# Who makes the low halves of the rotated queries and keys: two of four moved from VectorE to GpSimd

## The reference

```python
qkv = x @ Wqkv.T                         # 512 x 768
q, k, v = split(qkv)                     # 16 heads of 16 features
q = cos * q + rotate_half(q) * sin
k = cos * k + rotate_half(k) * sin
scores = q @ k.T / 4, causal, softmax
out = (scores @ v) @ Wo.T
```

## Time and profile before

| | |
|---|---|
| median of 3 runs | 2299.27 us (2298.2 to 2305.56) |
| profiled execution | 2291.23 us, its span 2289.5 us, granted TensorE clock 0.989 |
| instructions | 52,899 |
| busy: PE / DVE / ACT / POOL | 2109.5 (92%) / 1931.8 (84%) / 1354.4 (59%) / 1306.6 (57%) us |
| DMA queue | 291.90 MB, 50.3% of 16 engines |

### The profile page before, as it was taken

The page is one execution under the profiler, slowest core; times in us unless marked ns, Lnnn a source line. Parts: engine busy times, 40 slices in busy tenths (PEclk is TensorE's granted clock), DMA queues, the critical chain, the costliest instruction groups (busy, mean ns, idle before and its releaser), DMA issues.

```text
span 2289.5 us, 52899 instructions
## 1 busy us (share of the span) xinstructions
PE 2109.5 (92%) x17682; PEld 1141.4 (50%) x17682; DVE 1931.8 (84%) x4485; ACT 1354.4 (59%) x2568; POOL 1306.6 (57%) x1462
## 2 busy tenths in 40 slices
PE   4999999889999999999999999999999888999999
PEld 2666666434444444444444444444444434666666
DVE  6777788788999899999989998999999865777776
ACT  3455444266667666666666676666666655445553
POOL 6666667454555455456545554554555425666664
PEclk9999999899999999999999999999999999999999
DMA  6656666444445444444444454444445423666665
GB/s 208 192 192 207 201 203 200 116 89 89 98 95 101 94 94 98 89 94 93 99 89 100 95 101 94 96 92 96 93 94 98 99 70 118 197 202 194 204 207 167
DMA packets 280391, 295.29 MB, mean 129 GB/s; under 512 B 45784, under 2 KB 263224, under 8 KB 280120
## 3 DMA queue, kind: packets, MB, share of 16 engines
q1 hardware_dynamic: 280120, 291.90, 50.3%
HBM read 140.08 MB, written 83.89 MB: 98 GB/s over the span
## 4 chain that ended last, share of the span: by engine, by line
PE 45%; DVE 33%; SPq 7%; issue 6%; DMA 5%; ACT 4%; DVEq 0%; ACTq 0%
PE bank L710 8%; DVE bank L996 7%; DVE at_mx L1006 7%; PE bank L728 7%; PE bank L1185 6%; PE bank L1202 6%; PE bank L1219 4%; PE bank L1280 4%; ACT probs L1073 3%; DVE turned L975 3%; DVE v_qk L981 3%; DVE turned L974 2%; DVE at_stats L107 2%; PE bank L1255 2%; PE bank L1167 2%
## 5 line engine op out<-in xcount | busy, mean ns | idle before, releaser
L1073 ACT ACTIVATE probs<-bank 128x512 f32<-128x512 f32 x1280 | 747.0, 603 | 456.9 <-PE bank L1185 447.5
L912 POOL TENSOR_SCALAR_AFFINE_SELECT probs<-probs 128x512 f32<-128x512 f32 x512 | 320.4, 638 | 661.1 <-ACT probs L1073 659.3
L1006 DVE TENSOR_REDUCE at_mx<-bank 128x1 f32<-128x384 f32 (+2 forms) x896 | 509.6, 608 | 78.5 <-PE bank L1167 77.0
L1185 PE MATMUL bank<-stacks 49*128 49x512 f16 (+3 forms) x2048 | 458.7, 302 | 71.4 <-ACT probs L1073 71.0
L996 DVE CUSTOM_DVE_ANT_0 bank<-bank,xn 128x512 f32<-128x512 f32 x512 | 351.6, 698 | 38.8 <-PE bank L1158 36.2
L1185 PEld LDWEIGHTS bank<-stacks 49*128 49x128 f16 x2048 | 136.0, 94 | 458.6 <-ACT probs L1073 334.2
L1162 PE MATMUL bank<-stacks 48*128 48x384 f16 (+2 forms) x1536 | 307.7, 275 | 22.1 <-DVE at_mx L1006 15.6
L1167 PE MATMUL bank<-mask,turn 64*128 64x128 bf16 (+2 forms) x896 | 230.7, 257 | 0.0
L1158 PE MATMUL bank<-stacks 48*128 48x512 f16 x512 | 198.5, 389 | 10.6 <-DVE at_mx L996 6.4
L924 POOL TENSOR_TENSOR turned<-turned 128x512 f32<-128x512 f32 x128 | 184.7, 1443 | 19.1 <-POOL turned L920 0.4
L628 ACT ACTIVATE turned<-bank,b1s 128x512 f32<-128x512 f32 x128 | 88.2, 689 | 181.0 <-PE bank L710 179.3
(11 more groups left out here) (145 smaller groups left out, 4619.6 us busy)
## 6 DMA issues: line engine op xcount, KB each, us to landing
stacks<-qk_image SPq DMA_DIRECT2D x384, 128.0 KB, 4.5
qk_image<-v_qk SPq DMA_DIRECT2D x128, 256.0 KB, 3.7
stacks<-w_hi SPq DMA_DIRECT2D x192, 128.0 KB, 3.7
stacks<-w_lo SPq DMA_DIRECT2D x192, 128.0 KB, 3.8
b2s<-in_b SPq DMA_DIRECT2D x128, 128.0 KB, 3.9
after_ffn<-probs SPq DMA_DIRECT2D x32, 512.0 KB, 6.5
at_x<-after_ffn SPq DMA_DIRECT2D x32, 512.0 KB, 4.1
late_x<-after_ffn SPq DMA_DIRECT2D x32, 512.0 KB, 4.7
```

What stands on the lines that cost most here:

```text
L912: nc.gpsimd.affine_select(out=ap, in_=ap, compare_op=ALU.is_ge, fill=0.0, base=0, pattern=[[0, d] for d in dims] + [[1, P]], channel_multi ...
L1006: nc.vector.tensor_reduce(o_ap, i_ap, AX_X, ALU.max).then_inc(max_done, 1)
L1073: nc.scalar.activation(probs[:, c, :], st_ps[c % 2][:], ACT.Exp, scale=DH ** -0.5).then_inc(exp_done, 1)
L1185: ins = nc.tensor.matmul(bank[:, col:col + T - q0], k_stack[ss.par][rows, j + ha, kt * P:(kt + 1) * P], q_stack[ss.par][rows, j + ha, q0:T ...
```

## The change

The low halves of t = 0, 1 (queries) become GpSimd instructions in slot 1, each right behind the rotation steps of t = 2 and t = 3. The low halves of t = 2, 3 (keys) stay on VectorE in slot 2. To make that possible `rotated` gets four buffers; by_sin goes (the product with sin is made in place in swapped), so that the memory stays the same. The semaphore qk_lo becomes q_lo and k_lo; other users of qk_lo follow (not shown: L503, L620, L785, L1334).

```diff
-        rope = [[self.turned[:, 2 * j + i, :] for i in range(2)] for j in range(4)]
+        rope = [self.turned[:, 0:2, :], self.turned[:, 2:4, :], self.turned[:, 4:8, :]]
@@ SP, slot
             if g == 1 and sample(s + 1):
-                hold(sp, issue, qk_lo, 4 * n.b + 2)
+                hold(sp, issue, q_lo, 2 * n.b + 2)
                 (write q)
             if g == 2 and sample(s + 1):
                 (read q)
-                hold(sp, issue, qk_lo, 4 * n.b + 4)
+                hold(sp, issue, k_lo, 2 * n.b + 2)
                 (write k)
@@ GpSimd
-            nc.gpsimd.tensor_tensor(by_sin[t % 2][:], swapped[t % 2][:], sin_t[:], ALU.mult).then_inc(sin_done, 1)
-            wait(pool, qk_lo, idx - 1)
+            nc.gpsimd.tensor_tensor(swapped[:, t % 2, :], swapped[:, t % 2, :], sin_t[:], ALU.mult).then_inc(sin_done, 1)
+            wait(pool, q_lo if t < 2 else k_lo, 2 * n.b)
             pool.wait_ge(sin_done, idx + 1)
-            nc.gpsimd.tensor_tensor(rotated[t % 2][:], by_cos[t % 2][:], by_sin[t % 2][:], ALU.add).then_inc(rope_done, 1)
+            nc.gpsimd.tensor_tensor(rotated[:, t, :], by_cos[:, t % 2, :], swapped[:, t % 2, :], ALU.add).then_inc(rope_done, 1)
+
+        def q_low(n, t):
+            pool.wait_ge(qk_hi, 4 * n.b + t + 1)
+            wait(pool, q_written, 32 * n.b)
+            nc.gpsimd.tensor_tensor(qk.lo[:, t, :], rotated[:, t, :], qk.hi[:, t, :], ALU.subtract).then_inc(q_lo, 1)
@@ GpSimd, slot: mask 0, then
             if g < 2 and sample(s + 1):
                 rope(s + 1, 2 * g)
+            if g == 1 and sample(s + 1):
+                q_low(s + 1, 0)
                 (slot 2: normalise s + 2), masks 1 to 3, then
             if g < 2 and sample(s + 1):
                 rope(s + 1, 2 * g + 1)
+            if g == 1 and sample(s + 1):
+                q_low(s + 1, 1)
@@ VectorE
-        def rope_low(n, t):
+        def k_low(n, t):
             dve.wait_ge(qk_hi, 4 * n.b + t + 1)
-            wait(dve, q_written if t < 2 else k_written, 32 * n.b)
-            nc.vector.tensor_tensor(qk.lo[:, t, :], rotated[t % 2][:], qk.hi[:, t, :], ALU.subtract).then_inc(qk_lo, 1)
+            wait(dve, k_written, 32 * n.b)
+            nc.vector.tensor_tensor(qk.lo[:, t, :], rotated[:, t, :], qk.hi[:, t, :], ALU.subtract).then_inc(k_lo, 1)
@@ VectorE, slot
-                if g in (1, 2) and sample(s + 1) and n in (0, 3):
-                    rope_low(s + 1, 2 * (g - 1) + (n == 3))
+                if g == 2 and sample(s + 1) and n in (0, 3):
+                    k_low(s + 1, 2 + (n == 3))
```

More of the change, by code:

```diff
@@ L502, in residual @@
             if before and s == 0:
-                pool.wait_ge(before.qk_lo, 4 * B)
+                pool.wait_ge(before.k_lo, 2 * B)
             if before and s == 2:
@@ L619, in gelu @@
                 act.wait_ge(before.pv_done, 16 * (B - 1))
-                act.wait_ge(before.qk_lo, 4 * B)
+                act.wait_ge(before.k_lo, 2 * B)
             if before and s == 1:
@@ L759, in attention @@
     cos_t, sin_t = sb("cos", [P, T], F32), sb("sin", [P, T], F32)
-    q_stack, k_stack, v, qk, (swapped, by_cos, by_sin, rotated), ones = mem.of_attention()
+    q_stack, k_stack, v, qk, (swapped, by_cos, rotated), ones = mem.of_attention()
     x = mem.at_x
@@ L784, in attention @@
     xT_lo, qk_done, rope_in, sin_done = sem("xT_lo"), sem("qk_done"), sem("rope_in"), sem("sin_done")
-    rope_done, qk_hi, qk_lo, v_done = sem("rope_done"), sem("qk_hi"), sem("qk_lo"), sem("v_done")
+    rope_done, qk_hi, q_lo, v_done = sem("rope_done"), sem("qk_hi"), sem("q_lo"), sem("v_done")
+    k_lo = sem("k_lo")
     v_copied, mx_done, max_done, mt_done = sem("v_copied"), sem("mx_done"), sem("max_done"), sem("mt_done")
@@ L973, in begin_rope @@
             wait(dve, rope_done, idx - 1)
-            nc.vector.tensor_tensor(by_cos[t % 2][:], x_ps[t % 2][:], cos_t[:], ALU.mult)
-            nc.vector.stream_shuffle(swapped[t % 2][:], x_ps[t % 2][:], [i ^ 1 for i in range(32)]).then_inc(rope_in, 1)
-        def rope_low(n, t):
+            nc.vector.tensor_tensor(by_cos[:, t % 2, :], x_ps[t % 2][:], cos_t[:], ALU.mult)
+            nc.vector.stream_shuffle(swapped[:, t % 2, :], x_ps[t % 2][:], [i ^ 1 for i in range(32)]).then_inc(rope_in, 1)
+        def k_low(n, t):
             dve.wait_ge(qk_hi, 4 * n.b + t + 1)
-            wait(dve, q_written if t < 2 else k_written, 32 * n.b)
-            nc.vector.tensor_tensor(qk.lo[:, t, :], rotated[t % 2][:], qk.hi[:, t, :], ALU.subtract).then_inc(qk_lo, 1)
+            wait(dve, k_written, 32 * n.b)
+            nc.vector.tensor_tensor(qk.lo[:, t, :], rotated[:, t, :], qk.hi[:, t, :], ALU.subtract).then_inc(k_lo, 1)
         def maxima(s, g, n):
@@ L1078, in rope_high @@
             wait(act, q_written if t < 2 else k_written, 32 * n.b)
-            nc.scalar.activation(qk.hi[:, t, :], rotated[t % 2][:], ACT.Copy).then_inc(qk_hi, 1)
+            nc.scalar.activation(qk.hi[:, t, :], rotated[:, t, :], ACT.Copy).then_inc(qk_hi, 1)
         def high_of(hi, n, c, ps_done, hi_done):
@@ L1332, in attention @@
     own.xT_lo, own.rope_in, own.stored = xT_lo, rope_in, stored
-    own.st_done, own.pv_done, own.qk_lo, own.k_written = st_done, pv_done, qk_lo, k_written
+    own.st_done, own.pv_done, own.k_lo, own.k_written = st_done, pv_done, k_lo, k_written
     own.max_done, own.on_done, own.xn_done = max_done, on_done, xn_done
```

## The result

The changed kernel takes 2366.44 us (median of 4 runs, 2362.96 to 2372.5), the kernel before 2298.73 us (4 runs): ratio 1.0309, 95% interval 1.0276 to 1.0342 (an estimate over the single runs; the quotient of the two medians is 1.0295). It is slower, as forecast, and 3 us from the forecast of 2363. Most of the steps held, but one term of the sum is too large, and another cost, not foreseen, made up for it: that the number fits to 3 us is luck.

A forecast was written before the change was run, and what follows sets the result against it. PE (45%) and VectorE (33%) held the chain, the next sample's DRAM path nearly as late. A loop of 26.4 + 20.7 = 47.1 us against 45.04 adds 31 x 2.06 = 64 to 2291.2: 2355, plus 8 for the median, 2363 us; range 2318 to 2400.

The forecast's parts named there:

- VectorE's relief: Slots 1 and 2: VectorE is late by about 1.1 us a sample; giving that back vanishes in PE's wait.
- POOL's subtraction: Slot 1: each q low half on POOL takes 1.28 us, bounds 0.64 and 1.76.
- Q: POOL's slot 1: both q low halves are complete at 1224.5, 26.4 us after the start of slot 0.
- The DMA path from Q: q reads start at Q + 3.1, k writes at Q + 6.0, k reads at Q + 12.6, landed at Q + 20.7.
- The loop's period: Slot 0 to Q to the next slot 0: 47.1 us against 45.04, +2.06 us a sample.
- The sign that the prediction named for itself: Start of slot 0: a new PE wait of about 2 us once a sample, between DMA L846 and PE L1158 or L1162.
- The collision of the keys' low half with L920 of t = 3: Slot 2: by the port rule POOL's L920 can hold VectorE's key low half for a full 1.1 us.
- Rival 1: The DMA path fits in a loop of at most 44 us and VectorE's time counts: 2265 us at best, chance 0.09.
- Rival 2: The loop just closes at 44.8 to 45.3 us: no measurable change, 2299 us, chance 0.06.
- Rival 3: Slot 2's row of maxima, queued behind q writes, is late for slot 3: up to 0.7 us, 2287 us, chance 0.03.
- Rival 4: POOL is much slower at mixed types, 2.5 us each: period 49.5, +138 us, 2437 us, chance 0.05.

The follow-up runs named there:

- early_low_k_late: early_low with the keys' low half of t = 2 on VectorE moved behind maximum n = 2 of slot 2 instead of n = 0: 2254.10 us, ratio 0.9834.
- path_away: Changed kernel, but the DRAM image's low half of q is written from the high halves and SP waits for those only: 2349.51 us, ratio 1.0253.
- k_late: Changed kernel with only the keys' low half of t = 2 on VectorE moved behind maximum n = 2 of slot 2: 2343.65 us, ratio 1.0194.
- path_away_k_late: path_away with the keys' low half of t = 2 on VectorE moved behind maximum n = 2 of slot 2: 2293.77 us, ratio 1.0006.
- early_low: Changed kernel with POOL's q low halves moved forward in slot 1, t = 0 ahead of the first mask, t = 1 right behind it: 2296.86 us, ratio 1.0011.
- late_write: Changed kernel with all low halves back on VectorE, and SP also waiting for slot 2's first mask before writing q: 2421.69 us, ratio 1.0538.

## Why the prediction was right, and where it was not

- **VectorE's relief** (1.1 us a sample, to vanish in PE's wait): right in size. 0.76 us appeared in slot 1 and were lost again; early_low_k_late, without the new waits, gets 1.06, of which 0.74 are the q low halves' and 0.32 the reordering's.
- **POOL's subtraction** (1.28 us taken): 1.16 us, the median of 51 in the steady stretch (1149 to 1169 ns). It is a little faster than the float32 instructions beside it (1.27).
- **Q, the end of the q low halves** (26.4 us after the start of slot 0): 1170.26 - 1144.54 = 25.7. Two subtractions 0.12 shorter each and a collision of 0.27 instead of 0.45 are about 0.4 of the 0.7.
- **The DMA path from Q** (3.1, 6.0, 12.6 and 20.7 us): q reads at 1173.33 = Q + 3.1, k write at Q + 5.9, k reads at Q + 12.5, landed at 1190.55 = Q + 20.3. The k writes, issued 1.2 us earlier behind the reads (2.8 us after the first read for 4.03), landed no earlier, as taken: 9.4 us after the first read. In the seven samples with full clock and a wait for the stacks, PE starts 20.4 to 20.9 us after Q.
- **The loop's period** (47.1 us, +2.06): 46.1 in the sample shown, 46.1 to 46.6 in those seven, so +1.1 to +1.6. This is the term that was mis-sized. In the sample shown the error is the sum of the two above, 0.7 at Q and 0.3 behind it, small in themselves but half of the difference of two large numbers.
- **The clock** was not in the prediction at all, and costs the rest: a mean of 47.58 against 46.3 at full clock. The forecast of 2363 hit 2366 because the missing term (about 1.3 us a sample) covered what the loop was too long by (0.5 to 1.0). That is luck. The sign that the prediction named for itself, a new wait of about 2 us for the stacks once a sample, did not come: nine waits in 1100 us, 6.1 us in all.
- **The collision of the keys' low half with L920 of t = 3** stood in the prediction as 1.1 us for VectorE by a rule, and then went into the sum only as 0.4 us for POOL. It happened as described, VectorE's timeline of the changed kernel:

```profile
1166.69 1.30 DVE L992 TENSOR_TENSOR v_qk<-turned,v_qk 128x512 f16<-128x512 f32 x1
...
1170.46 0.65 DVE L115 TENSOR_SCALAR at_ve<-at_pair 128x4 f32<-128x4 f32 x1
```

with POOL's:

```profile
1166.17 1.27 POOL L921 TENSOR_TENSOR turned<-turned,at_sin 128x512 f32<-128x512 f32 x1
1167.60 1.54 POOL L925 TENSOR_TENSOR turned<-turned 128x512 f32<-128x512 f32 x1
1169.10 1.15 POOL L931 TENSOR_TENSOR v_qk<-turned,v_qk 128x512 f16<-128x512 f32 x1
1170.45 0.63 POOL L913 TENSOR_SCALAR_AFFINE_SELECT probs<-probs 128x512 f32<-128x512 f32 x1 [0.20 <-ACT probs L1084]
```

The low half began 0.5 us into L921 and ended 0.55 us after it: 1.30 us for 0.69. Then L115 ran beside the mask that POOL started at 1170.45 (0.63 us) and ended with it, at 1171.1. The two cost VectorE 0.61 and 0.48 us on PE's way to its n = 5, and PE waited 1.42 us there. In the prediction's loop such a delay costs nothing. In a sample with a wait for the stacks that is so: it took 1.24 us of slot 2, and left only 0.63 us for the wait at the stacks, where "about 2 us" were forecast. But this is the wait behind which the clock fell, and in the samples with a low stretch PE is mostly later than the path. The two causes overlap: remove the path (path_away) and 1.0253 remains, make the collision smaller (k_late) and 1.0194 remains, do both (path_away_k_late) and the loss is gone, 1.0006, as it is in early_low.
- **Rival 1** (the path fits, and VectorE's time counts, 2265 us): wrong for this kernel, but it is what early_low_k_late does, with 2254. **Rival 2** (no measurable change): excluded by the interval. **Rival 3** (the row of maxima late): it goes out at 1171.32, long before its use at 1177; no sign of it. **Rival 4** (slow mixed types): excluded by the 1.16 us.

The Trainium skill (SBUF — State Buffer, the shared port pair) names two kinds of VectorE instruction that are excluded by a running GpSimd instruction, those with two SBUF inputs and those in a 2-port mode. Of the first kind the traces show two sizes, 1.30 for 0.69 us (L992, changed kernel) and 1.13 for 0.16 us (L113, path_away_k_late). L115, with one input, was held too (0.65 us for 0.17), which agrees with the second kind if such an instruction runs in that mode; no run here shows the mode itself.

How the 71.7 us of span (2361.2 less 2289.5) divide can't be given as a sum of three. By the means a sample, samples at full clock explain 1.2 of the 2.54 us and the clock the other 1.3. Within the 1.2 the causes overlap: at full clock the samples of path_away are 0.5 us longer than before, those of k_late 1.1 on average (45.3 to 47.2 us).

## What to carry to other kernels

A step moved to an idle engine is paid for by what waits for its result, so trace the result to its last reader before the move, DMAs and the queue order of their issuer included, and put the step at the earliest gap of the new engine instead of behind its other work: here the same two instructions cost 68 us placed late and nothing placed early, and together with one reordering on VectorE they win 38. Before VectorE and GpSimd work share a stretch, list VectorE's instructions there that read SBUF twice, the tiny ones too, since each can stand behind a whole GpSimd instruction. When the period is a difference of long paths, price PE's new waits also by the clock.

## What the runs showed of the hardware that I had not expected

A wait of PE of 1.4 us once in 46 us, in slot 2 of path_away, was followed within 2 us by a stretch of 3.4 to 10.2 us at 1.2 GHz in 14 of 26 samples; waits of 1.11 us (early_low) at the same place were in 1 of 26, waits of 0.93 us (path_away_k_late) in none. The length of the wait alone does not decide it: in late_write six waits of 1.3 to 2.1 us for the stacks had no such stretch behind them. The same program (path_away) with 1.3 us more PE work in that gap ran 44 us faster. And a VectorE instruction on 4 elements took 1.13 us beside a GpSimd subtraction.
